# A hybrid layer stack on one Trainium2 core: the second router's logits from kept products, and a new order of the convolution's pieces

## What is computed

```python
x = x + _L0_attn_a_ref(_layernorm(x), ...)   # selective scan over the sequence
x = x + _L0_ffn_ref(_layernorm(x), ...)      # mixture of 8 experts
x = x + _L0_attn_b_ref(_layernorm(x), ...)   # long convolution (Hyena)
x = x + _L0_ffn_ref(_layernorm(x), ...)      # the same mixture again
```

## Time and profile before

| | |
|---|---|
| median of 3 runs | 494.86 us (494.80 to 494.87) |
| profiled execution | 495.49 us |
| its span | 493.7 us |
| TensorE busy | 292.3 us, 59% |
| VectorE busy | 343.4 us, 70% |
| ScalarE busy | 212.3 us, 43% |
| GpSimd busy | 309.2 us, 63% |

### The profile page before, as it was taken

The page is one execution under the profiler, slowest core; times in us unless marked ns, Lnnn a source line. Parts: engine busy times, 40 slices in busy tenths (PEclk is TensorE's granted clock), DMA queues, the critical chain, the costliest instruction groups (busy, mean ns, idle before and its releaser), DMA issues.

```text
span 493.7 us, 4946 instructions
## 1 busy us (share of the span) xinstructions
PE 292.3 (59%) x1327; PEld 152.8 (31%) x1327; DVE 343.4 (70%) x794; ACT 212.3 (43%) x346; POOL 309.2 (63%) x218
## 2 busy tenths in 40 slices
PE   4978753588877887970010782439778584036730
PEld 3323310312412412530000551216355583024410
DVE  4798699999999999977260763453787974236520
ACT  2787755246556646511010491334785121015610
POOL 2142189699999999957575002767745647527674
PEclk9999975587787777685555798566799896559965
DMA  7014240840100100106412342110201122132200
GB/s 212 18 69 129 60 127 0 285 195 0 43 0 0 44 0 1 44 1 174 110 44 77 110 152 74 54 43 27 68 13 33 56 66 93 38 110 80 78 23 11
DMA packets 29159, 34.12 MB, mean 69 GB/s; under 512 B 5488, under 2 KB 20862, under 8 KB 29132
## 3 DMA queue, kind: packets, MB, share of 16 engines
q1 hardware_dynamic: 24236, 25.39, 16.7%
q0 software_dynamic: 4096, 7.71, 4.9%
q10 hardware_dynamic: 800, 0.71, 0.5%
HBM read 14.43 MB, written 20.19 MB: 70 GB/s over the span
## 4 chain that ended last, share of the span: by engine, by line
DVE 26%; issue 26%; PE 20%; POOL 8%; ACT 6%; another core or an unknown queue 5%; DMA 3%; DVEq 3%; SPq 2%; ACTq 1%; POOLq 0%
DVE states L825 13%; POOL x L1157 3%; POOL states L810 2%; PE ps L1521 2%; PE ps L1592 2%; ACT scaled L1257 2%; PE ps L1611 2%; PE ps L1062 2%; DVE stats L882 1%; PE ps L691 1%; POOL slots L1036 1%; PE ps L1195 1%; SPq L1409 1%; PE ps L1211 1%
## 5 line engine op out<-in xcount | busy, mean ns | idle before, releaser
L810 POOL TENSOR_TENSOR states<-states,c_rows 128x1024 f32<-128x1024 f32 x60 | 144.5, 2440 | 18.2 <-DVE states L825 17.8
L825 DVE TENSOR_TENSOR_SCAN states<-ps,inp 128x1024 f32<-128x1024 f32 x64 | 140.5, 2261 | 0.4 <-ACT ps L786 0.4
L786 ACT ACTIVATE ps<-ps,bias_p,scale_p 128x1024 f32<-128x1024 f32 x64 | 75.0, 1177 | 64.5 <-PE ps L676 64.2
L1036 POOL DMA_INDIRECT slots<-x,put x64 | 63.9, 999 | 47.1 <-DVE put L1030 28.8
L676 PE MATMUL ps<-stack,sel 96*128 96x512 bf16 x128 | 49.6, 482 | 35.3 <-DVE states L825 35.1
L1157 POOL DMA_INDIRECT x<-answers,put x32 | 30.9, 965 | 45.5 <-DMA answers<-reply 36.5
L1348 POOL DMA_INDIRECT out<-reply,home x32 | 31.6, 988 | 24.9 <-DVE reply L1327 17.0
L691 PE MATMUL ps<-states,red 128*32 128x512 f32 x256 | 41.6, 764 | 2.5 <-POOL states L810 2.5
L1327 DVE SCALAR_TENSOR_TENSOR reply<-ps,rows,kept 128x128 f32<-128x128 f32 x64 | 18.6, 344 | 29.7 <-remote 18.0
L676 PEld LDWEIGHTS ps<-stack,sel 96*128 96x128 bf16 x128 | 8.8, 104 | 75.7 <-DVE states L825 64.7
L882 DVE BATCH_NORM_STATS2 stats<-x 128x6 f32<-128x128 f32 x96 | 19.8, 277 | 14.1 <-DMA x<-answers,put 13.9
(11 more groups left out here) (174 smaller groups left out, 604.5 us busy)
## 6 DMA issues: line engine op xcount, KB each, us to landing
slots<-zero SPq DMA_DIRECT2D x8, 528.0 KB
rows<-slots SPq DMA_DIRECT2D x16, 264.0 KB
steps<-part SPq DMA_DIRECT2D x4, 768.0 KB, 3.3
stack<-steps SPq DMA_DIRECT2D x12, 256.0 KB, 4.2
answers<-x SPq DMA_DIRECT2D x4, 512.0 KB
answers<-reply SPq DMA_DIRECT2D x8, 256.0 KB, 2.6
out<-x SPq DMA_DIRECT2D x4, 512.0 KB
x<-in_x SPq DMA_DIRECT2D x3, 512.0 KB, 5.6
```

The lines of the kernel that those rows point to most:

```text
L786: act.activation(bank(ps, slot(b, u), 2), bank(ps, slot(b, u), 2), ACT.Exp, scale=m["scale_p"][:, group(u):group(u) + 1], bias=m["bias_p"] ...
L810: eng.tensor_tensor(h[:, u * SEQ:(u + 1) * SEQ], h[:, u * SEQ:(u + 1) * SEQ], c_rows[:, b * SEQ:(b + 1) * SEQ], ALU.mult).then_inc(done, 1)
L825: dve.tensor_tensor_scan(h[:, u * SEQ:(u + 1) * SEQ], bank(ps, slot(b, u), 2), inp[:, b * SEQ:(b + 1) * SEQ], 0.0, ALU.mult, ALU.add).then ...
L1036: pool.indirect_dma_start(out=m["slots"][n // BATCH], out_offset=bass.IndirectOffsetOnAxis(m["put"][:, b, i:i + 1], 0), in_=m["x"][:, b * ...
```

## The change

1. The second router's logits are no longer made from the new rows. They are split: the old rows' part comes from the normalised, transposed rows `xt` that the convolution has anyway (`old_logits`, TensorE; `take_logits`, ScalarE), divided by the convolution's inverse deviation (`carry`, VectorE). The convolution's part comes from `z` with the product of `w_out` and the router's weights, `w_z`, and from `b_out` (`new_logits`, TensorE, right behind `output`; the two together are `outcome`). `choose` adds the two, and waits for the deviations only after that.
2. `w_z` is made once at the start (`join_tensor`, `join_scalar`): two transposes, a product, two copies.
3. The router's transposes and their copies go, with the buffer `rx_t`.
4. The order is new on all engines: on TensorE `streams(3)` are together and behind `outcome(1)` and block 0's counts; on ScalarE block 0's exponentials stand behind all of `take_streams` and `first_tap` of block 3, and `deviations(1)` behind `v_copy(0)`; on VectorE block 1's first statistics are split around the taps of block 0, the router's statistics of block 0 stand ahead of the convolution's of block 3, and each `place` directly follows its `choose`; on GpSimd four gathers move ahead of `bias(0)`.

The core of the diff:

```diff
-    def transpose(self, pe, n, ready=None, count=0):
-        b = n % BATCH
-        self.tr.transpose(pe, "r", n, self.m["x"][:, b * BT:(b + 1) * BT, 0:D], ready, count)
-
-    def copy(self, act, n):
-        need(act, self.logit_psum, n - BATCH - 1)
-        self.tr.copy(act, "r", n, self.m["rx_t"][:, n % 2, :])
-
-    def logits(self, pe, n):
-        self.tr.need_copy(pe, "r", n)
-        need(pe, self.logit_read, n - BATCH)
-        for i in range(BT):
-            last = pe.matmul(self.ps[:, self.LOGITS * HALF + i * EXPERTS:self.LOGITS * HALF + (i + 1) * EXPERTS],
-                             self.m["rx_t"][:, n % 2, i * P:(i + 1) * P], self.m["w_r"][:, :], start=True, stop=True)
-        last.then_inc(self.logit_psum, 1)
+    def carry(self, dve, n):
+
+        m, b = self.m, n - BATCH
+        tiles = slice(b * BT, (b + 1) * BT)
+        old = m["row_logit"][:, b, :].rearrange("p (i e) -> p i e", e=EXPERTS)
+        dve.wait_ge(self.old_logits, 2 * b + 2 + CREDIT)
+        dve.reciprocal(m["total"][:, :], m["rstd"][:, 1, tiles])
+        dve.drain()
+        dve.tensor_tensor(old, old, m["total"][:, :].rearrange("p (i o) -> p i o", o=1).broadcast_to([P, BT, EXPERTS]), ALU.mult)
+        dve.drain()
...
-        dve.wait_ge(self.row_rstd, n + 1 + CREDIT)
+        row = m["row_logit"][:, b, :].rearrange("p (i e) -> p i e", e=EXPERTS)
         if n < BATCH:
             dve.wait_ge(m["logits_taken"], n + 1 + CREDIT)
-            dve.tensor_tensor(m["logit"][:, :, :], m["row_logit"][:, n, :].rearrange("p (i e) -> p i e", e=EXPERTS), spread_out, ALU.mult)
         else:
             dve.wait_ge(self.logit_psum, n - BATCH + 1 + CREDIT)
-            dve.tensor_tensor(m["logit"][:, :, :], bank(self.ps, self.LOGITS)[:, 0:BT * EXPERTS].rearrange("p (i e) -> p i e", e=EXPERTS),
-                              spread_out, ALU.mult).then_inc(self.logit_read, 1)
+            dve.tensor_tensor(row, row, bank(self.ps, self.LOGITS)[:, 0:BT * EXPERTS].rearrange("p (i e) -> p i e", e=EXPERTS),
+                              ALU.add).then_inc(self.logit_read, 1)
+            dve.drain()
+        dve.wait_ge(self.row_rstd, n + 1 + CREDIT)
+        dve.tensor_tensor(m["logit"][:, :, :], row, spread_out, ALU.mult)
...
+    def join_tensor(self, pe):
+        ident = self.m["const"][:, C_ID:C_ID + P]
+        pe.transpose(self.ps[:, HALF:HALF + D], self.w_out[:, :], ident)
+        pe.transpose(self.ps[:, HALF + D:HALF + 2 * D], self.b_out[:, :], ident).then_inc(self.join_psum, 1)
+        need(pe, self.joined, 1)
+        pe.matmul(self.ps[:, HALF:HALF + EXPERTS], self.w_out_t[:, 0, :], self.m["w_r"][:, :], start=True, stop=True).then_inc(self.join_psum, 1)
+        need(pe, self.joined, 2)
+
+    def join_scalar(self, act):
+        need(act, self.join_psum, 1)
+        act.copy(self.w_out_t[:, :, :], by_tile(self.ps[:, HALF:HALF + 2 * D])).then_inc(self.joined, 1)
+        need(act, self.join_psum, 2)
+        act.copy(self.w_z[:, :], self.ps[:, HALF:HALF + EXPERTS]).then_inc(self.joined, 1)
...
+    def old_logits(self, pe, b):
+
+        at = self.tr.at("a", b)
+        for h in range(2):
+            need(pe, self.tr.left, at - 3 + h)
+            for i in range(HT):
+                last = pe.matmul(self.ps[:, h * HALF + i * EXPERTS:h * HALF + (i + 1) * EXPERTS],
+                                 self.xt[:, b % 2, (h * HT + i) * P:(h * HT + i + 1) * P], self.m["w_r"][:, :], start=True, stop=True)
+            last.then_inc(self.tr.full, 1)
+
+    def take_logits(self, act, b):
+        at, n = self.tr.at("a", b), HT * EXPERTS
+        for h in range(2):
+            need(act, self.tr.full, at - 1 + h)
+            act.copy(self.m["row_logit"][:, b, h * n:(h + 1) * n], self.ps[:, h * HALF:h * HALF + n]).then_inc(self.tr.left, 1)
+            act.sem_inc(self.router.old_logits, 1)
+
+    def new_logits(self, pe, b):
+
+        router, at = self.router, self.router.LOGITS * HALF
+        need(pe, router.logit_read, b)
+        pe.matmul(self.ps[:, at:at + BT * EXPERTS], self.w_out_t[:, 1, :],
+                  self.m["w_r"][:, :].rearrange("p (o e) -> p o e", o=1).broadcast_to([P, BT, EXPERTS]), start=True, stop=False)
+        for i in range(BT):
+            last = pe.matmul(self.ps[:, at + i * EXPERTS:at + (i + 1) * EXPERTS], self.z[:, b % 2, i * P:(i + 1) * P], self.w_z[:, :],
+                             start=False, stop=i == BT - 1)
+        last.then_inc(router.logit_psum, 1)
...
-        def route(b):
-            router.transpose(pe, second(b), conv.x_done, b + 1)
-            router.logits(pe, second(b))
+        def outcome(b):
+            conv.output(pe, b)
+            conv.new_logits(pe, b)
...
         streams(1)
-        conv.output(pe, 0)
+        outcome(0)
+        conv.old_logits(pe, 0)
         normal_rows(2)
         streams(2)
         convolve(1)
-        router.transpose(pe, second(0), conv.x_done, 1)
+        conv.old_logits(pe, 1)
         normal_rows(3)
-        router.logits(pe, second(0))
-        conv.streams(pe, 3, 0)
+        outcome(1)
         router.count(pe, second(0))
-        conv.streams(pe, 3, 1)
-        conv.output(pe, 1)
+        streams(3)
         convolve(2)
-        route(1)
-        conv.output(pe, 2)
+        conv.old_logits(pe, 2)
+        conv.old_logits(pe, 3)
+        outcome(2)
         router.count(pe, second(1))
-        conv.v_transpose(pe, 3)
-        router.transpose(pe, second(2), conv.x_done, 3)
-        conv.long_conv(pe, 3)
-        router.logits(pe, second(2))
-        conv.output(pe, 3)
+        convolve(3)
+        outcome(3)
         router.count(pe, second(2))
-        route(3)
         router.count(pe, second(3))
...
         conv.first_tap(act, 1)
+        conv.take_logits(act, 0)
         conv.normalize(act, 2)
         conv.copy(act, 2)
         conv.take_streams(act, 2, 0)
@@ -1747,25 +1795,23 @@
         conv.take_streams(act, 2, 1)
         conv.first_tap(act, 2)
         conv.v_copy(act, 1)
+        router.row_deviations(act, second(0))
         conv.normalize(act, 3)
-        router.row_deviations(act, second(0))
-        router.copy(act, second(0))
+        conv.take_logits(act, 1)
         conv.copy(act, 3)
         conv.take_streams(act, 3, 0)
-        router.probabilities(act, second(0))
         conv.take_streams(act, 3, 1)
         conv.first_tap(act, 3)
+        router.probabilities(act, second(0))
         conv.v_copy(act, 2)
-        router.copy(act, second(1))
         router.row_deviations(act, second(1))
+        conv.take_logits(act, 2)
+        conv.take_logits(act, 3)
         router.probabilities(act, second(1))
         conv.v_copy(act, 3)
-        router.copy(act, second(2))
-        router.row_deviations(act, second(2))
-        router.probabilities(act, second(2))
-        router.copy(act, second(3))
-        router.row_deviations(act, second(3))
-        router.probabilities(act, second(3))
+        for b in range(2, BATCH):
+            router.row_deviations(act, second(b))
+            router.probabilities(act, second(b))
         experts.scalar(act, 1)
...
         conv.statistics(dve, 0)
         conv.taps(dve, 0, 0)
-        conv.statistics(dve, 1)
+        conv.statistics_half(dve, 1, 0)
         conv.taps(dve, 0, 1)
+        conv.statistics_half(dve, 1, 1)
         conv.shift(dve, 1)
...
         conv.add(dve, 0)
+        router.statistics(dve, second(0))
         conv.statistics(dve, 3)
-        router.statistics(dve, second(0))
         conv.shift(dve, 3)
+        router.carry(dve, second(0))
         conv.taps(dve, 2)
         conv.gate_y(dve, 1)
         routed(0)
         added(1)
         conv.taps(dve, 3)
         conv.gate_y(dve, 2)
-        router.choose(dve, second(1))
-        conv.add(dve, 2)
-        router.place(dve, second(1))
-        router.statistics(dve, second(2))
+        router.carry(dve, second(1))
+        routed(1)
+        added(2)
+        router.carry(dve, second(2))
         conv.gate_y(dve, 3)
-        router.choose(dve, second(2))
-        conv.add(dve, 3)
-        router.place(dve, second(2))
-        router.statistics(dve, second(3))
+        routed(2)
+        router.carry(dve, second(3))
+        added(3)
         routed(3)
...
         experts.gather(pool, 2, 1)
+        experts.gather(pool, 3, 0)
         conv.bias(pool, 0)
-        experts.gather(pool, 3, 0)
         experts.gather(pool, 3, 1)
```

31 lines of the change are left out of this document (20 added, 11 removed).

## The result

Six executions of the changed kernel have a median of 508.08 us (503.23 to 509.93), beside 494.83 us of the kernel before (490.83 to 500.8): a ratio of 1.0276 with a 95% interval of 1.0208 to 1.0345, **slower**, as forecast, by 13.2 us where the sum said 10.0. The profiled execution took 509.93 us around a span of 508.1 us.

What follows compares the result with a forecast made beforehand. It saw a chain across VectorE, TensorE and waits as the bound, deciding when GpSimd starts block 3's scatters. That start's +8.1 us plus lateness of 1.3 and 0.6 gave +10.0 on the 494.86 median: 504.9 us, range 498 to 512.

Steps and rivals of the forecast that it cites:

- z(1): End of block 1's second gate step on VectorE: 1.5 us later, at 373.1, bounded by 3 us either way.
- taps(3): Start of block 3's convolution taps on VectorE: at 390.2 us, against 383.41 before.
- z(2): End of block 2's second gate step on VectorE, held by GpSimd's product: 400.8 us, 8.0 later.
- z(3): End of block 3's second gate step on VectorE: 413.8 us, against 405.30 before.
- scatters(3) start: GpSimd starts block 3's scatters once block 2's are out: 433.7 us against 425.62, +8.1.
- lateness: Unexplained late VectorE starts near the end: 1.3 us on the last counts, 0.6 ahead of block 2's counts.
- The wait for the exponentials: VectorE, after choosing for block 0, idles for ScalarE's exponentials, now behind block 3's streams and first taps: 6.8 us bare.
- the head: Block 0's second-half taps no longer wait behind statistics needing the last gathers: convolution starts up to 3 us earlier.
- block 3's convolution is ready by 410.0: TensorE finishes block 3's transposes (1.0 us), copy and products (3.42) by 410.0, before VectorE's gate steps.
- The tail: Block 3's output, new logits and block 2's counts at TensorE's half rate: 7.9 us, against 4.1 at full rate.
- rival (b): Half rate already from block 2's output and new logits on, and lateness of 4.2: +16, 511 us; chance 0.19.
- The setup: Joining the weights, some 2 us bare, lies in TensorE's 6.65 us wait for the filter taps and costs nothing.

Runs made afterwards that it cites:

- e1: Changed kernel with block 3's stream matmuls put ahead of block 1's output and new logits and block 0's counts on TensorE; ratio 1.0183 to the kernel before.
- e2: Changed kernel with block 0's exponentials put ahead of block 3's stream copies and first taps on ScalarE; ratio 1.0289 to the kernel before.
- e3: Kernel before with only the change's new order at the head (split statistics, earlier copies of v(0), earlier gather); ratio 0.9993 to the kernel before.
- e4: Changed kernel's algebra with every step in the order of the kernel before; ratio 1.0129 to the kernel before.
- e7: Changed algebra and head; streams, exponentials, statistics and adds in old places, new logits behind the next block's convolution, carry ahead of gates; ratio 1.0081 to the kernel before.
- e10: e7 plus, on TensorE, block 0's old logits ahead of its output and its new logits behind block 1's convolution; ratio 1.0077 to the kernel before.
- e6: Changed kernel with the new logits of blocks 1, 2 and 3 behind the counts and next block's convolution on TensorE; ratio 1.0148 to the kernel before.
- e9: Changed kernel with block 3's statistics ahead of the router's again, and block 0's old and new logits moved as in e10; ratio 1.0333 to the kernel before.

## Why the prediction was right, and where not

All as differences to before, the right columns from the first gather on:

| step | predicted | first profile | second |
|---|---|---|---|
| z(1) | +1.5 | +3.7 | +3.7 |
| taps(3) | +6.8 | +8.9 | +8.9 |
| z(2) | +8.0 | +7.1 | +7.1 |
| put(1) | +6.5 | +9.4 | +7.5 |
| z(3) | +8.5 | +13.7 | +12.2 |
| scatters(2) start | +11.6 | +14.6 | +13.3 |
| scatters(3) start | +8.1 | +11.1 | +9.8 |
| behind the last scatter, lateness | +1.9 | -1.3 | -1.1 |
| ahead of the first gather | 0 | +4.6 | -0.45 |
| span | +10.0 | +14.4 | +8.2 |

**The wait for the exponentials** is right in mechanism and size: 6.8 us bare, 8.08 seen, and z(1) to taps(3) took 17.0 us where the prediction had 390.2 - 373.1 = 17.1. e1 and e2 show it is the cause.

**z(1)** was mis-sized. Block 1's convolution begins 1.4 us later in both profiles, about the +1.5 that the prediction gave z(1) as a whole; but then it takes 5.80 and 5.24 us where it took 3.50, at a granted clock of 0.59 and 0.66 where it was 1.00. That term, 2.3 and 1.7 us, is not in the sum, and with it z(1) falls outside its bounds of 3 us. Of the effects that are, the swapped statistics measured about 1 us, against the 2.6 read from the rows, and the head gave z(1) nothing in e3. **z(2)**: the step that had GpSimd's product hold the second gate step did not happen. The scatters of block 0 ran until 404.1, the gate (403.22, 1.23 us) had begun before the product did, and the product held the carry's second step instead, 2.10 us against the 0.23 of others. The wait for an add, which the prediction missed, stands here too: TensorE was idle for 5.55 us ahead of block 2's convolution until the add of block 1 was through.

```profile
394.33 5.91 PE L1614 MATMUL ps<-toep,c_vt 128*128 128x256 f32 x18 [5.55 <-DVE x L1669]
```

No loss from it is seen, since that convolution ended at 400.2 and VectorE's taps at 401.9.

**z(3) is the step that failed**: "block 3's convolution is ready by 410.0", which is 9.2 us behind z(2). It was ready 16.5 and 14.9 us behind it:

| from z(2), us | predicted | first profile | second |
|---|---|---|---|
| output, new logits, counts | 4.1 | 7.6 | 5.7 |
| transposes and copies | 1.7 | 2.6 | 1.8 |
| more wait for the add | 0 | 0.5 | 1.3 |
| convolution | 3.4 | 5.7 | 6.1 |

The larger part is TensorE's rate. The sum had the full rate up to z(3), and the half rate only behind it; but over the output and new logits of block 2 the granted clock was 0.50 in the first profile, 0.57 and 0.87 in the second, and over the convolution 0.60 and 0.56. The smaller part is the wait for the add, which the prediction had moved in VectorE's list without its reader on TensorE. Part of both was hidden, since VectorE itself was given until 411.2: 13.0 us were given from z(2) to z(3), and it took 19.1 and 17.6. That the new logits hold z(3) is shown by e4 (17.2 with the add in time), and by e7 and e10 (13.9 and 13.6 with both edits). How much the add alone would hold is not shown: e6, which was to show it, delayed block 2's output.

**The tail**: rival (b) had the half rate from block 2's outcome on, and that half of it came true (3.78, 0.53 and 3.53 us in the first profile); the outcome of block 3 got 7.9 us and took 5.7 (counts read at 429.24, z(3) at 423.55), since the granted clock was 0.57 over its output's products and 1.00 over most of its logits. From z(3) to scatters(3) the prediction gave 19.9 us, 17.7 were needed: that pays back part of z(3). **Lateness**, 1.9 us, was not there; in the second profile of the kernel before it was hardly there either, so it belonged to the execution. **The setup** cost nothing, as said. The median is 3.2 us above the forecast: +1.7 to +3.0 in the stage up to the last scatters, -3 behind it, and a first stage at the half clock in most of the six executions, whose times lie at 503.2 and 504.0 and at 507.7 to 509.9; the two that were profiled of the unedited kernel took 509.93 with the half clock and 503.68 without. That the four long ones all had it is argued, not seen. So the sum came near in part by luck: 3.7 to 5.2 us too little at z(3) stand against 2.0 to 2.2 too much in the tail and 3 too much behind the last scatter.

Of the signs, VectorE's idle time (8.08 us, 6 to 9 named), the put lists that wait for counts (2.14 and 2.43 us in the first profile) and the scatters of blocks 2 and 3 back to back (0.30 us between them) came; block 3's taps came 8.9 us later after the first gather, not 5 to 8. The loss is in the stage: behind the last scatter the changed kernel needs 57.0 us, not more than before.

## What to carry to other kernels

When a step moves in a queue, look for who waits for *every* result it leaves, a freed bank too: the add was costed, its reader was not. Work that is moved out of one wait lands in another: the new logits moved alone gave 0.6 us from z(2) to z(3), because they came to stand ahead of the next output; with the add and the streams in their old places, 3.7. Give a stretch of TensorE both its lengths in the sum: block 1's convolution took 3.50 us and 5.80. And an algebraic saving must be counted on the engine that pays for it: eight transposes of 1.06 us were traded for nine small products of 2.08. Last, compare two profiles from an event that both have: the first gather lay anywhere from 297.8 to 309.1 us in kernels that share all but the setup ahead of it.

## What the runs showed of the hardware

TensorE's granted clock in the first stage falls towards the half (0.57 to 0.69 over 44 to 48 us in five profiles, with TensorE busy all of the time) in some executions and stays at 1.00 in others, of one and the same kernel. The first gather comes 4.5 to 4.8 us later with it than in a profile of the kernel before of the same speed. The same happens in the stage itself: block 1's convolution took 3.50 us in e10 and 5.18 in e9, with the same steps ahead of it, and TensorE had stood 2.73 and 3.36 us; after 2.73 us it also took 5.17, in e7. So the idle time just ahead of it does not tell the rate. In the sessions in which before took 494 us, readers of TensorE's results begin late by the rows: the changed kernel's join transposes end at 263.51 + 0.42 = 263.93, and their reader begins 2.8 us behind, at 266.69. In the sessions with 481 us the same wait ahead of block 3's choice is 1.01 instead of 5.18 us. The granted clock does not explain this, and its cause stays open.

```profile
263.51 0.42 PE L1437 MATMUL ps<-const,c_b_out 128*128 128x128 f32 x1
```

```profile
266.69 0.37 ACT L1444 COPY c_w_out_t<-ps 128x256 f32<-128x256 f32 x1 [4.45 <-remote]
```

VectorE's L886, 0.17 us where it is alone, took 4.24 us in the changed kernel: from 359.22 to the end of two GpSimd additions (358.77 + 4.65 = 363.42). Carry's L940 (2.10) likewise ended with GpSimd's product (404.13 + 2.52 = 406.65). Block 3's taps ran in 5.03 us wholly beside scatter issues.

```profile
359.22 4.24 DVE L886 TENSOR_SCALAR spread<-moments 128x8 f32<-128x8 f32 x1
```

```profile
358.77 4.65 POOL L1593 TENSOR_TENSOR x<-x,c_b_out 128x1024 f32<-128x1024 f32 x2
```

The Trainium skill (SBUF — State Buffer, section "SBUF: two separate sides") has this lock on the shared port pair, held for a whole instruction, for VectorE instructions with two SBUF inputs or in a 2-port mode. For tensor operations the traces agree, with the numbers above, but L886 waited through two GpSimd instructions in a row. No run shows that L886, which has one input, was in such a mode. For the scatter issues, which this section doesn't set apart, the 5.03 us of the taps show no lock.
